# A stage list in another order, with the expert scores copied out a stage earlier in the last two batches

## What is computed

```python
x = x + L0_xattn(layernorm(x), ctx, mask)      # 8 heads of 64, softmax over 64 context rows
x = x + L0_ffn(layernorm(x))                   # 16 experts of 64, each token's best 4, relu
x = x + L1_xattn(layernorm(x), ctx)            # top-32 attention (4 heads), FiLM, s4d, FFN, norm
x = x + L1_ffn(x)                              # 8 experts; each takes its best 512 of all 4096 tokens
```

## Time and profile before

| | us |
|---|---|
| time, median of 3 runs | 1424.18 |
| the profiled execution | 1421.83 |
| its span, first to last instruction | 1420.0 |
| TensorE busy | 1231.5 (87%) |
| VectorE busy | 922.0 (65%) |
| ScalarE busy | 479.5 (34%) |
| GpSimd busy | 340.1 (24%) |

### The profile page before, as it was taken

The page is one execution under the profiler, slowest core; times in us unless marked ns, Lnnn a source line. Parts: engine busy times, 40 slices in busy tenths (PEclk is TensorE's granted clock), DMA queues, the critical chain, the costliest instruction groups (busy, mean ns, idle before and its releaser), DMA issues. The chain is left out here.

```text
span 1420.0 us, 17680 instructions
## 1 busy us (share of the span) xinstructions
PE 1231.5 (87%) x5325; PEld 743.2 (52%) x5325; DVE 922.0 (65%) x3415; ACT 479.5 (34%) x860; POOL 340.1 (24%) x603
## 2 busy tenths in 40 slices
PE   5776967998999899799989979999687439999996
PEld 3543544555466465455546635554364326667764
DVE  6767897778768767777867877797974581111110
ACT  3534431163153326215332531532412422322221
POOL 4223220033023112202212220320203222322331
PEclk9787978999999999999989999999898659999999
DMA  9002003000300300210030030021000135433421
GB/s 289 25 15 61 19 1 76 18 1 17 90 19 1 106 18 1 61 46 18 15 91 18 1 97 25 3 61 38 1 0 1 61 111 165 143 90 90 96 37 18
DMA packets 45353, 72.54 MB, mean 51 GB/s; under 512 B 8549, under 2 KB 27208, under 8 KB 45130
## 3 DMA queue, kind: packets, MB, share of 16 engines
q1 hardware_dynamic: 39114, 62.88, 15.0%
q0 software_dynamic: 6144, 8.52, 3.4%
HBM read 58.27 MB, written 13.07 MB: 50 GB/s over the span
## 5 line engine op out<-in xcount | busy, mean ns | idle before, releaser
L835 POOL TENSOR_SCALAR ve<-mv 128x2 f32<-128x2 f32 x74 | 16.9, 228 | 515.2 <-DVE mv L1103 515.1
L1675 PE MATMUL ps<-x,keys 128*128 128x512 f32 x256 | 124.4, 610 | 1.8 <-DVE hT L1197 1.8
L1840 PE MATMUL ps<-hT,values 128*128 128x512 f32 x256 | 120.0, 598 | 0.0
L2290 PE MATMUL experts_ps<-experts_yT,experts_fc 128*128 128x512 f32 x256 | 113.4, 601 | 1.2 <-ACT experts_yT L2215 1.2
L2302 PE MATMUL experts_ps<-experts_fc,experts_hT 128*128 128x256 f32 x512 | 112.0, 379 | 0.8 <-ACT experts_hT L2227 0.8
L1675 PE MATMUL ps<-zT_second,w 128*128 128x512 f32 x224 | 104.5, 606 | 6.2 <-ACT big L1616 3.9
L2302 PEld LDWEIGHTS experts_ps<-experts_fc,experts_hT 128*128 128x128 f32 x512 | 96.7, 190 | 14.5 <-ACT experts_hT L2227 1.6
L1675 PE MATMUL ps<-w,big 128*128 128x256 f32 x448 | 99.0, 379 | 0.8 <-ACT big L1616 0.8
L2199 DVE SCALAR_TENSOR_TENSOR experts_o<-experts_ps,experts_wh,experts_b2w 128x256 f32<-128x256 f32 x32 | 15.5, 484 | 128.7 <-PE experts_ps L2302 128.7
L2227 ACT ACTIVATE experts_hT<-experts_ps,experts_b 128x512 f32<-128x512 f32 x64 | 44.0, 687 | 156.9 <-PE experts_ps L2290 156.9
L1675 PEld LDWEIGHTS ps<-w,big 128*128 128x128 f32 x448 | 84.1, 190 | 12.5 <-ACT big L1616 1.6
(11 more groups left out here) (445 smaller groups left out, 2448.1 us busy)
## 6 DMA issues: line engine op xcount, KB each, us to landing
gT<-expert_gates SPq DMA_DIRECT2D x32, 512.0 KB, 7.9
experts_fc<-in_fc1T SPq DMA_DIRECT2D x8, 1024.0 KB, 5.1
experts_fc<-in_fc2T SPq DMA_DIRECT2D x8, 1024.0 KB, 8.6
xT<-in_xT SPq DMA_DIRECT2D x8, 512.0 KB, 3.6
x<-in_x SPq DMA_DIRECT2D x8, 512.0 KB, 3.5
expert_table<-tb SPq DMA_DIRECT2D x7, 528.0 KB, 9.9
out_x<-x SPq DMA_DIRECT2D x7, 512.0 KB, 9.2
w<-in_W SPq DMA_DIRECT2D x2, 1024.0 KB, 9.5
```

Of the source, the lines that this page charges most:

```text
L835: nc.gpsimd.tensor_scalar(o, i, c, None, ALU.add).then_inc(*tick(*event))
L1675: last = nc.tensor.matmul(o, l, r_, start=start, stop=stop)
L1840: last = nc.tensor.matmul(bank("O2", k), S["values"][:, c, k * P:(k + 1) * P], hT[:, c % RING, :], start=(c == 0), stop=(c == HC - 1))
L2290: last = nc.tensor.matmul(g_bank(m), fc1[e % 3][:, k, m * P:(m + 1) * P], yT[e % 2][:, k, :], start=(k == 0), stop=(k == DC - 1))
```

## The change

The list is written in another order, for every batch. The same stages stand in it, each once, and two names are new. `scales` is the second part of GpSimd's `scores`, and stands directly behind it everywhere. `scores_out` is PE's `table` and the last part of ACT's `table`, the wait for `ST` and the copy. In batches 0 to 5 the list has `table` and then `scores_out`; in batches 6 and 7 `scores_out` and then `table`.

```diff
             def scores(b, h):
+                w = room(b)
+                rstd_of(b, LN_EXPERTS, h, w)
+
+            def scales(b, h):
                 ts = pair(h)
                 w = room(b)
                 tr, tmr, tnm, tv, ts2, tnm2 = w.scale
-                rstd_of(b, LN_EXPERTS, h, w)
...
                     nc.scalar.activation(x3[:, t, :], x3[:, t, :], ACT.Identity, bias=w.tnm[:, t, :], scale=w.tr[:, t, :]).then_inc(*tick("x4", t))
+
+            def scores_out(b):
+                w = room(b)
                 a.wait_ge(*w.uses.at(b, "filled", "ST"))
...
-            def table(b):
+            def scores_out(b):
                 w = room(b)
                 pe.wait_ge(*at(b, "sc1"))
```

Parts of the list that the prediction speaks of, old and then new. The first is the middle of the start, the second the hand-over with batch 3's attention sum, the third the end:

```diff
-    (KERN, 0, "powers", 3), (MID, 0, "text", 0), (MID, 0, "relu", 0), (KERN, 0, "phases", 5), (MID, 0, "mlp", 2),
-    (MID, 0, "text", 1), (MID, 0, "relu", 1), (MID, 0, "relu", 2), (MID, 0, "mlp", 3), (KERN, 0, "film_split"), (MID, 0, "relu", 3),
...
-    (ATTEND, 1, "attend", 1), (MID, 0, "pick", 1, 0), (ATTEND, 1, "attend", 2), (MID, 0, "shift"), (ATTEND, 1, "soften", 2),
-    (MID, 0, "pick", 1, 1), (KERN, 0, "powers", 6), (KERN, 0, "powers", 7), (MID, 0, "pick", 1, 2), (MID, 0, "pick", 1, 3),
+    (KERN, 0, "powers", 3), (MID, 0, "relu", 0), (MID, 0, "text", 0), (MID, 0, "mlp", 2), (MID, 0, "mlp", 3), (MID, 0, "relu", 1),
+    (MID, 0, "mlp", 4), (KERN, 0, "phases", 5), (MID, 0, "relu", 2), (KERN, 0, "powers", 4), (MID, 0, "mlp", 5), (MID, 0, "mlp", 6),
+    (KERN, 0, "fold_film"), (MID, 0, "mlp", 7), (MID, 0, "relu", 3), (MID, 0, "mlp", 8), (MID, 0, "relu", 4), (KERN, 0, "phases", 6),
...
+    (ATTEND, 1, "attend", 2), (ATTEND, 1, "soften", 2), (KERN, 0, "film_split"), (KERN, 0, "powers", 6), (KERN, 0, "powers", 7),
+    (MID, 0, "pick", 1, 0), (MID, 0, "pick", 1, 1), (MID, 0, "pick", 1, 2), (MID, 0, "pick", 1, 3), (MID, 0, "pick", 2, 0),
+    (MID, 0, "pick", 2, 1), (KERN, 0, "kernel", 0), (MID, 0, "shift"), (MID, 0, "pick", 2, 2), (MID, 0, "rows", 0),
```

```diff
-    (MID, 2, "pick", 3, 3), (LAST, 1, "norm_out", 1), (ATTEND, 3, "attend_sum"), (LAST, 1, "scores", 1), (MID, 2, "picked", 0),
-    (ATTEND, 3, "route"), (ATTEND, 3, "gates", 0), (ATTEND, 3, "turn_route"), (ATTEND, 3, "gates", 1), (ATTEND, 3, "gates", 2),
-    (LAST, 1, "route_experts"), (ATTEND, 3, "gates", 3), (MID, 2, "text", 2), (LAST, 2, "film_in", 0), (LAST, 1, "shift_scores"),
-    (MID, 2, "picked", 1), (LAST, 2, "film_in", 1), (LAST, 2, "film", 0), (LAST, 1, "turn_scores"), (ATTEND, 3, "spread"),
+    (MID, 2, "pick", 2, 2), (LAST, 1, "ffn_add", 1), (MID, 2, "pick", 2, 3), (LAST, 1, "norm_out", 1), (ATTEND, 3, "attend_sum"),
+    (ATTEND, 3, "attend_out"), (ATTEND, 3, "route"), (ATTEND, 3, "turn_route"), (MID, 2, "pick", 3, 0), (LAST, 1, "scores", 0), (LAST, 1, "scales", 0),
+    (LAST, 1, "scores", 1), (LAST, 1, "scales", 1), (MID, 2, "pick", 3, 1), (LAST, 1, "route_experts"), (ATTEND, 3, "gates", 0), (MID, 2, "picked", 0),
+    (ATTEND, 3, "gates", 1), (ATTEND, 3, "gates", 2), (MID, 3, "mlp", 0), (ATTEND, 3, "gates", 3), (MID, 2, "pick", 3, 2),
+    (MID, 2, "pick", 3, 3), (MID, 2, "picked", 1), (LAST, 1, "turn_scores"), (MID, 2, "text", 2), (LAST, 1, "shift_scores"),
+    (LAST, 2, "film_in", 0), (LAST, 2, "film_in", 1), (ATTEND, 3, "spread"), (MID, 3, "relu", 0), (MID, 3, "relu", 1),
```

```diff
-    (LAST, 6, "scores", 1), (LAST, 7, "gelu", 7), (LAST, 6, "shift_scores"), (LAST, 6, "route_experts"), (LAST, 7, "ffn_out", 0),
-    (LAST, 6, "turn_scores"), (LAST, 7, "ffn_out", 1), (LAST, 7, "norm_out", 0), (LAST, 7, "ffn_add", 1), (LAST, 6, "table"),
-    (LAST, 7, "scores", 0), (LAST, 7, "norm_out", 1), (LAST, 7, "shift_scores"), (LAST, 7, "scores", 1), (LAST, 7, "route_experts"),
-    (LAST, 7, "table"),
+    (LAST, 7, "gelu", 7), (LAST, 6, "route_experts"), (LAST, 7, "ffn_out", 0), (LAST, 6, "turn_scores"), (LAST, 7, "ffn_out", 1),
+    (LAST, 7, "norm_out", 0), (LAST, 7, "ffn_add", 1), (LAST, 6, "shift_scores"), (LAST, 6, "scores_out"), (LAST, 6, "table"), (LAST, 7, "scores", 0), (LAST, 7, "scales", 0),
+    (LAST, 7, "norm_out", 1), (LAST, 7, "shift_scores"), (LAST, 7, "scores", 1), (LAST, 7, "scales", 1), (LAST, 7, "route_experts"), (LAST, 7, "scores_out"), (LAST, 7, "table"),
```

More of the change, by code:

```diff
@@ L123 @@
     (KERN, 0, "steps", 0), (KERN, 0, "steps", 1), (ATTEND, 0, "keys", 0), (KERN, 0, "centre", 0), (KERN, 0, "centre", 1),
[L124 to L131, removed]
@@ L212 @@
-    (ATTEND, 4, "gates", 1), (LAST, 2, "shift_scores"), (ATTEND, 4, "gates", 2), (LAST, 2, "table"), (MID, 4, "mlp", 1),
-    (ATTEND, 4, "spread"), (ATTEND, 4, "gates", 3), (MID, 3, "picked", 1), (LAST, 3, "film_in", 0), (LAST, 3, "film_in", 1),
-    (LAST, 3, "film", 0), (MID, 4, "relu", 0), (LAST, 3, "fold"), (MID, 4, "relu", 1), (LAST, 3, "film", 1), (LAST, 3, "transform"),
-    (MID, 4, "text", 0), (MID, 4, "relu", 2), (LAST, 3, "turn"), (LAST, 3, "product", 0), (LAST, 3, "product", 1), (MID, 4, "mlp", 2),
@@ new lines @@
+    (LAST, 0, "scores", 0), (LAST, 0, "scales", 0), (LAST, 0, "ffn_add", 1), (MID, 1, "picked", 0), (ATTEND, 2, "attend_sum"), (MID, 1, "pick", 3, 3),
+    (LAST, 0, "norm_out", 1), (ATTEND, 2, "gates", 0), (LAST, 0, "scores", 1), (LAST, 0, "scales", 1), (MID, 2, "mlp", 0), (ATTEND, 2, "gates", 1),
+    (ATTEND, 2, "gates", 2), (ATTEND, 2, "gates", 3), (MID, 1, "text", 2), (LAST, 0, "route_experts"), (MID, 1, "picked", 1),
+    (LAST, 1, "film_in", 0), (LAST, 0, "shift_scores"), (ATTEND, 2, "spread"), (LAST, 1, "film_in", 1), (LAST, 0, "turn_scores"),
@@ new lines @@
+    (ATTEND, 5, "route"), (ATTEND, 5, "turn_route"), (ATTEND, 5, "gates", 1), (ATTEND, 5, "gates", 2), (LAST, 3, "scores", 1), (LAST, 3, "scales", 1),
+    (ATTEND, 5, "gates", 3), (MID, 4, "picked", 1), (MID, 5, "mlp", 0), (MID, 4, "text", 2), (LAST, 4, "film_in", 0),
+    (LAST, 3, "shift_scores"), (ATTEND, 5, "spread"), (LAST, 3, "route_experts"), (LAST, 4, "film_in", 1), (LAST, 4, "film", 0),
+    (LAST, 3, "turn_scores"), (LAST, 4, "film", 1), (MID, 5, "relu", 0), (MID, 5, "mlp", 1), (LAST, 3, "table"), (LAST, 3, "scores_out"), (LAST, 4, "fold"),
@@ new lines @@
+    (ATTEND, 6, "attend_sum"), (MID, 5, "picked", 0), (LAST, 4, "scores", 0), (LAST, 4, "scales", 0), (ATTEND, 6, "gates", 0), (MID, 5, "pick", 3, 2),
+    (LAST, 5, "film", 0), (ATTEND, 6, "gates", 1), (ATTEND, 6, "gates", 2), (LAST, 4, "scores", 1), (LAST, 4, "scales", 1), (LAST, 4, "route_experts"),
+    (ATTEND, 6, "gates", 3), (ATTEND, 6, "spread"), (LAST, 4, "turn_scores"), (LAST, 4, "table"), (LAST, 4, "scores_out"), (MID, 5, "pick", 3, 3),
+    (LAST, 5, "film_in", 0), (MID, 6, "mlp", 0), (LAST, 5, "film", 1), (LAST, 4, "shift_scores"), (MID, 5, "picked", 1),
@@ new lines @@
+    (LAST, 5, "ffn_out", 0), (ATTEND, 7, "spread"), (ATTEND, 7, "gates", 3), (MID, 6, "picked", 0), (LAST, 5, "ffn_add", 0),
+    (MID, 6, "pick", 3, 2), (LAST, 5, "ffn_add", 1), (LAST, 5, "norm_out", 0), (LAST, 5, "norm_out", 1), (LAST, 5, "ffn_out", 1),
+    (MID, 6, "pick", 3, 3), (MID, 7, "mlp", 0), (MID, 7, "relu", 0), (MID, 6, "text", 2), (LAST, 5, "scores", 0), (LAST, 5, "scales", 0), (MID, 6, "picked", 1),
+    (MID, 7, "mlp", 1), (LAST, 5, "scores", 1), (LAST, 5, "scales", 1), (LAST, 6, "film_in", 0), (MID, 7, "relu", 1), (MID, 7, "relu", 2), (LAST, 6, "film", 0),
```

311 lines of the change are left out of this document (151 added, 160 removed).

## The result

The changed kernel takes 1440.57 us (median of 4 runs, 1440.43 to 1446.33), the kernel before 1425.15 us (4 runs, 1421.99 to 1427.73): a ratio of 1.0119, with a 95% interval of 1.0086 to 1.0152. It is slower, by 1.2%. The forecast was 1426 us with a range up to 1440. The profiled execution has a span of 1438.6 us, 18.6 more than before; the medians lie 15.4 apart, since the profiled execution of the kernel before (1421.83 us) was as fast as the fastest of its four runs. All that follows on single stretches is read from the profiled executions.

What follows compares the result with a forecast made beforehand. VectorE was taken as busier in the start, TensorE as bounding the middle, no engine as full in the tail. Tail −0.3, start +2.5 and middle −0.4 gave +1.8: 1423.6 us, 1426 on the median's footing, range 1408 to 1440.

Steps and rivals of the forecast that it cites:

- The split of the stages: `scores` on GpSimd and `table` in batches 0 to 5: instructions stay in the same order or adjacent, 0 us.
- Batch 7's copy: Tail, ScalarE: the scores are copied ahead of the row operations, so the threshold search starts 2.45 us sooner.
- Batch 6's copy: Tail, ScalarE: copy and row operations come ahead of batch 7's transposed-row copies, +3.2 us, bounds 0 and +5.
- The tail's −1.0 for the earlier transform: Batch 7's film and transform move ahead of part of batch 6's feed-forward, sooner by about 1.0 us.
- The start: Up to batch 0's first transform: three moves and the text and clock given back, together +2.5 us, between −3 and +9.
- the ordering of keys: Start: named among changes in the walk through VectorE's list that ends batch 0's `film_in` 4 to 6 us later; no separate price.
- −0.6 "of 3.8": Start: `film_split` leaves `phases` 5; only 0.6 of 3.8 us counted as gained, as TensorE's expert products set the end.
- `film_split` beside `powers` 6: Start: the overlap of GpSimd and VectorE priced at 1 us, between 0 and +3.8.
- 1.0 us of `text` around the wait: Start: `text` 0 and 1 of batch 1 stand around TensorE's wait for `film_in`, giving back 1.0 us.
- The middle: Six middle batches: hand-overs sum to +1.6 us, clock −2, together −0.4, between −15 and +10.
- the waits at the hand-overs are filled: Rival, middle: a third of all waiting (14 us) goes, time about 1410 us; chance 0.31.
- The start passes on its delay: Rival, start: late `film_in` of batch 0 starts the first transform 9 us later; with hand-over 3, +12, 1436 us; chance 0.27.

Runs made afterwards that it cites:

- f1: The kernel before, its old list with the two stages split and batch 7's copy of the scores ahead of the row operations; 1418.84 us, 0.9969.
- f2: f1 with `film_split` moved ahead of batch 1's first attention pieces, beside picks 0.0 to 0.3; 1416.41 us, 0.9954 to the kernel before.
- f3: The changed kernel with batch 6's `shift_scores`, row operations and copy back in their old places and order; two runs, 1441.1 and 1443.4 us.
- e4: The changed kernel with `keys` 1, `centre` 2 and `centre` 3 of the start where they were before; 1438.02 us, 1.0093 to the kernel before.
- g2: The old list with only `centre` 2, `keys` 1 and `centre` 3 put ahead of `powers` 0; 1425.17 us, 1.0013 to the kernel before.
- g3: The old list with only `film_split` put ahead of `powers` 6 and `shift` behind pick 2.1; 1425.50 us, 1.0008 to the kernel before.
- e2: The changed kernel with `film_split` alone moved ahead of batch 1's first attention pieces, beside picks; 1436.51 us, 1.0080 to the kernel before.
- e3: The changed kernel with `text` 0 of batch 1 behind batch 0's transform, as before; 1443.41 us, 1.0122 to the kernel before.
- g1: The changed kernel with the edits of e2, e4 and f3 together; 1431.78 us, 1.0058 to the kernel before.
- e1: The changed kernel with the stages ahead of batch 0's transform in old order and `text` 0 of batch 1 behind it; 1432.94 us, 1.0067 to the kernel before.

## Why the prediction was wrong

*The split of the stages (0)*: right; no time is seen there.

*Batch 7's copy (−2.45)*: right. From `route_experts` to the end of the copy it gains 2.46 us in the changed kernel (22.90 us later at the one, 20.44 at the other), and the row operations beside the search cost nothing (f1, f2).

*Batch 6's copy (+3.2)*: right in mechanism and size: 2.9 (19.99 us later at `ffn_out`, 22.90 at the end of the copies of batch 7's transposed rows), and 2.85 back in f3.

*The tail's −1.0 for the earlier transform*: it came, and more. TensorE is 20.3 us later than before at the first feed-forward products of batch 6, 18.4 at batch 7's transform, whose `film` now stands further ahead among them, and 16.9 behind it. Of these 3.4 us, 1.6 are luck: the transform ran in 3.62 us for 5.18, at the higher clock. What I had not priced lies on both sides of it: 1.9 lost ahead of those products, and 3.1 behind, where the transposes of batch 6 had been moved ahead of batch 7's first `gelu` and wait 1.87 us for their norm, and 1.6 more go by the lower clock. The tail is +2.0, not −0.3. (By its own terms the tail's lower bound was −3.45 and not −4.5.)

*The start (+2.5, bounds −3 to +9)* is the step that failed first. It was 13.9 at the transform, 10.9 at `film_in`, where the walk had 4 to 6. Four terms:

- The order ahead of `powers` 0 stood in it as "the ordering of keys" without a price. On ScalarE a copy, two evacuations and a wait came ahead of the exponential that the whole chain through `powers` 0 to 5 hangs on: 3.5 us there, 4.5 at the first relu, all of which e4 and g2 carry to `film_in`. In the changed kernel itself 3.3 of it is hidden, because `film_split` left `phases` 5.
- That gain was set at −0.6 "of 3.8" as TensorE would set the end; at batch 0's last product it was 3.2 to 3.4 (g3, f2).
- `film_split` beside `powers` 6 was set at 1 between 0 and 3.8. It was 5.2. The upper end had come from four of the six stretched operations, and the argument for a low value, that picks stand there, was wrong: GpSimd is done before them. The sentence on the rule of the Trainium skill, "SBUF — State Buffer", "Who interferes with whom", pointed to the high end, and the runs bear it out: the additions with two SBUF inputs were held up, 2.50 us for 0.69 in the changed kernel, and took 0.69 again in e2.
- The "1.0 us of `text` around the wait" was wrong in sign at the transform: text and transform wait for the same `film_in`. For the work behind, it made no difference (e3).

With `film_split` and the order ahead of `powers` 0 both undone (g1), 8.8 of the 10.9 us come back at `film_in`; the last 2.1 are not explained by a run.

*The middle (−0.4)* is the other step that failed. By `film_in` it was +7.5, and it is the same in the changed kernel and in e1, with its old start. The walk went through VectorE's list alone ("only what stands between the attention sum and `film_in` 1 of a hand-over does") and looked for a gain at the clock. What grew was TensorE's waiting, 49.8 us for 42.3, and above all that of `spread` for the gates (12.4 for 4.2), as TensorE's own order at the hand-overs had changed. Of the signs set for it, 704 to 720 us held, at 719.0, and 35 to 45 us of waiting was missed, at 49.5. The separation is the same in all profiles: 41.6 to 42.8 us of waiting in the five kernels with the old list in the middle, 49.1 to 51.0 in the eight with the new one, while TensorE's busy time overlaps (674.3 to 680.8 and 679.1 to 683.2). That the middle lost mainly by waits and not by the clock is thus shown; that the place of `spread` is the reason is read from lists and traces, and no run moves it alone.

The single hand-overs in us, as forecast and as measured from one `film_in` to the next (hand-over n ends with `film_in` n−1):

| hand-over | 2 | 3 | 4 | 5 | 6 | 7 |
|---|---|---|---|---|---|---|
| forecast | +0.3 | +3.2 | −1.2 | −1.3 | +0.6 | 0 |
| measured | +2.7 | +1.1 | +3.0 | +0.1 | −0.9 | +1.5 |

Two of these differences hold in all profiles: hand-over 2 takes 124.0 to 124.7 us with the new list and 119.1 to 121.7 with the old, hand-over 7 takes 119.0 and 117.5. The reading that VectorE's order is unchanged is right for hand-over 4 (its work there comes 16.43 us later up to `picked`) and wrong for 7, where one pick was moved ahead of the attention sum and two behind the gates; and at hand-over 5 one `text` part stood ahead of the transform already. The 3.0 of hand-over 4 are the clock, and lie within what the old list shows there.

*The rivals*: "the waits at the hand-overs are filled" saw the right waits, those for `amT`, and they fell by 5.5 us; others grew by more. "The start passes on its delay" named the right place, `film_in` of batch 0, and its point of decision held, with a price of the start above its upper end. But that its 1436 us came near 1440.6 is in part luck, as it has none of the middle's loss. The sum by experiments: the start cost 7.6 us in time (1440.57 less e1's 1432.94), and the rest of the list 9.7 (e1 less the 1423.2 of before). In the profiles of e1 and before, 7.7 of the latter lie between `film_in` 0 and `film_in` 6, and 2 in the tail. The start's price also belongs to this list: in the old one the same two moves of the start, made singly, cost 1 us or less by the medians (g2, g3).

## What to carry to other kernels

When a list of stages is moved, walk the engine that is off the critical path too: a short stage of it that goes ahead of the one operation a long chain waits for costs its time and its own wait, to the end of that chain. Walk the engine that sets the length of the stretch as well, wait by wait: a stage taken from in front of a wait makes the wait longer, even where the engines it waits for do what they did. Before a stage is put into a gap, look up what both sides of the gap wait for; a filler that waits for the same thing fills nothing. And price an overlap of VectorE and GpSimd by the two instructions, not by their engines alone.

## What the runs showed of the hardware that was not expected

TensorE's clock can fall in full work as well. In e3 the scores of batch 2's text ran in 9.37 us with TensorE busy throughout and the clock at 0.50, the lower of its two levels. TensorE had been busy for 36.93 of the 37 us before, at the full clock. The same products in the changed kernel took 5.16. e3:

```profile
417.87:427.24 9.37, 9.37 (x22) 5.63 (x22) 4.44 (x32) 2.55 (x6) 4.34 (x6) 0.50 0.18 60
```

The changed kernel:

```profile
415.82:420.98 5.16, 5.16 (x23) 3.43 (x23) 4.47 (x31) 2.55 (x6) 3.32 (x6) 1.00 0.40 121
```

The list is the same in both from 260 us on; e3 came 1.6 to 2.1 us later from there to this stretch. So one order doesn't have one clock. From transform 0 to 6 the old order took 724.9 us in the kernel before and 719.6 in g2, and eight runs of the kernel before lie 9.7 us apart (1419.94 to 1429.62). Single waits moved as the list says, by 2.46 and 2.85 us at the copies for 2.45 and 2.9 expected; what the clock adds or takes elsewhere is as large as these gains.
